# Fill products on TensorE and re-spaced side work in a tile-by-tile cross attention

## The reference

```python
q = (x @ Wq + bq).reshape(1, B * N, H, hd)          # 1024 queries, 16 heads of 16
kv = (cond @ Wkv + bkv).reshape(1, -1, 2, H, hd)    # 1024 keys, all batches together
q = _fq_sym(q * scale, axis=-1)     # scale 1/4; rounded to 255 steps per row and head
k = _fq_sym(k, axis=-1)
v = _fq_sym(v, axis=2)
attn = softmax(einsum('bhqd,bhkd->bhqk', q, k))
attn = _fq_unsigned(attn, axis=-1)  # rounded to 256 steps of the row's maximum
out = einsum('bhqk,bhkd->bhqd', attn, v)
return out.reshape(B, N, C) @ Wp + bp
```

## Time and profile before

| | |
|---|---|
| median of 3 executions | 662.7 us (661.12 to 663.51) |
| the profiled execution, its own time | 660.63 us |
| its span | 658.7 us |
| TensorE matmuls busy | 468.4 us (71%) |
| VectorE busy | 455.1 us (69%) |
| ScalarE busy | 299.2 us (45%) |
| GpSimd busy | 269.0 us (41%) |
| mean granted TensorE clock | 0.723 |

### The profile page before, as it was taken

One profiled execution on the slowest core, in us unless ns is written; L12 is line 12 of the kernel. 1 busy time (PEld: TensorE's weight loads), 2 busy tenths in 40 slices (PEclk: granted clock), 3 DMA queues, 4 the chain that ended last, 5 costly groups with the idle time before them and its releaser, 6 DMA issues.

```text
span 658.7 us, 9547 instructions
## 1 busy us (share of the span) xinstructions
PE 468.4 (71%) x3244; PEld 263.3 (40%) x3244; DVE 455.1 (69%) x930; ACT 299.2 (45%) x526; POOL 269.0 (41%) x335
## 2 busy tenths in 40 slices
PE   2966825648888785989989989999995147555640
PEld 1525612436455553334343434343333136444430
DVE  6797999878469769897878887878893842211003
ACT  1453113544400644876767676767772103323320
POOL 6441659884250553032221212121110047888870
PEclk9988876977789998555565755565555557999885
DMA  8640000007000001979877896979997198885556
GB/s 306 186 158 1 0 0 1 0 12 117 1 1 1 2 3 33 173 133 159 136 145 151 143 159 132 153 141 162 167 162 187 22 321 211 200 218 91 86 68 205
DMA packets 187247, 74.87 MB, mean 114 GB/s; under 512 B 159232, under 2 KB 184768, under 8 KB 187200
## 3 DMA queue, kind: packets, MB, share of 16 engines
q1 hardware_dynamic: 181056, 65.35, 46.3%
q0 software_dynamic: 6144, 8.92, 7.7%
HBM read 27.56 MB, written 8.93 MB: 55 GB/s over the span
## 4 chain that ended last, share of the span: by engine, by line
PE 37%; DVE 36%; issue 9%; DMA 8%; POOL 5%; ACT 3%; SPq 0%; POOLq 0%; DVEq 0%; ACTq 0%
PE ps L968 9%; DVE nm L1356 8%; PE ps L907 5%; DMA sums<-A,slot_token 4%; DVE AT L1274 4%; PE ps L897 4%; PE ps L747 3%; PE ps L978 3%; DMA A<-x_rows,slot_token 3%; POOL A L571 2%; POOL sums L585 2%; PE ps L902 2%; PE ps L846 1%; PE ps L766 1%; DVE AT L1146 1%
## 5 line engine op out<-in xcount | busy, mean ns | idle before, releaser
L700 ACT ACTIVATE A<-ps,b,sq 128x1024 int16<-128x1024 f32 x128 | 154.0, 1203 | 72.1 <-DVE b L1360 66.8
L1356 DVE TENSOR_REDUCE nm<-ps 128x1 f32<-128x1024 f32 x128 | 155.4, 1214 | 7.9 <-PE ps L968 7.2
L968 PE MATMUL ps<-big,ctx_sb 64*128 64x512 bf16 x256 | 124.0, 587 | 15.0 <-ACT A L700 12.5
L978 PEld LDWEIGHTS ps<-VI,A 128*128 128x128 f16 x1024 | 37.2, 105 | 99.9 <-issue 94.9
L1466 DVE TENSOR_TENSOR AT<-AT,ps 128x128 f32<-128x128 f32 x32 | 9.2, 287 | 84.1 <-ACT AT L717 70.2
L519 POOL TENSOR_SCALAR veps<-mv 128x1 f32<-128x1 f32 (+1 forms) x15 | 3.5, 233 | 149.2 <-DVE mv L1288 149.2
L585 POOL DMA_INDIRECT sums<-A,slot_token x32 | 51.5, 1608 | 15.4 <-issue 8.6
L978 PE MATMUL ps<-VI,A 128*128 128x16 f16 x1024 | 48.6, 176 | 3.8 <-DMA A<-A 3.8
L571 POOL DMA_INDIRECT A<-x_rows,slot_token x32 | 34.5, 1078 | 32.6 <-DVE slot_token L1456 23.1
L1047 PE MATMUL ps<-identf,A 128*128 128x128 f32 x64 | 15.3, 325 | 37.8 <-DMA A<-x_rows,slot_token 37.7
L711 ACT ACTIVATE A<-ps 128x256 f32<-128x256 f32 x32 | 12.2, 383 | 58.7 <-PE ps L1047 57.0
(11 more groups left out here) (271 smaller groups left out, 996.6 us busy)
## 6 DMA issues: line engine op xcount, KB each, us to landing
A<-in SPq DMA_DIRECT2D x32, 256.0 KB
A<-in SPq DMA_DIRECT2D x32, 128.0 KB
A<-in SPq DMA_DIRECT2D x2, 1024.0 KB, 14.8
sums<-zeros SPq DMA_DIRECT2D x4, 512.0 KB, 4.7
A<-A SPq DMA_TRANSPOSE x128, 3.3
A<-sums SPq DMA_DIRECT2D x8, 256.0 KB, 4.6
X<-in SPq DMA_DIRECT2D x1, 1024.0 KB, 5.8
big<-in SPq DMA_DIRECT2D x1, 1024.0 KB, 8.5
```

Source lines behind the costliest of these rows:

```text
L700: a.activation(Y5[:, n % YB, :], ps[:, 2 * (n % 3):2 * (n % 3) + 2, :], ACT.Exp, scale=sq5[:, q, h:h + 1], bias=b5[:, n % 4:n % 4 + 1], ac ...
L968: done = T.matmul(ps[:, 2 * (n % 3) + c, :], QT5[rows, q % 3, h // 2, :], KT5[rows, h // 2, c * 512:(c + 1) * 512], start=True, stop=True)
L978: done = T.matmul(ps[:, 6 + q % 2, h * HD:(h + 1) * HD], PT5h[:, m % YB, k, :], VI[:, k, h * HD:(h + 1) * HD], start=(k == 0), stop=(k == 7))
L1356: v.tensor_reduce(nm5[:, n % 4:n % 4 + 1], ps[:, 2 * (n % 3):2 * (n % 3) + 2, :].rearrange("p a c -> p (a c)"), AX.X, ALU.max, negate=True ...
```

## The change

- In each of the 128 units in which no side product is issued, TensorE makes two products of 256 columns of the identity with stored keys, into a part of a bank that nothing reads.
- The side products move. The order of a block was: transpose 1, wp 3, out_proj 5, transpose of tile q - 1 at 7, of tile q + 2 at 9, router 10, queries 12. It is now: transpose 2, out_proj 4, wp 6, transpose of tile q + 2 at 8, queries 10, transpose of tile q - 1 at 12, router 14. The order of the layer norms and of what GpSimd and SyncE do follows it.
- The bias of the queries is added by a product of one row on TensorE ahead of the query projection; ScalarE copies the queries and the logits out of PSUM, which VectorE did before.
- The factor 1/4 is left out of the reciprocal and multiplied into the scale, on GpSimd for tiles 2 to 7, and the first head of a tile waits for it on VectorE and ScalarE.

The diff (left out: the order of the layer norms, the declaration of LG5 in a free part of A, and its use by the router):

```diff
@@ -282,11 +283,12 @@
             q, rest = (n - LAG5) // H, (n - LAG5) % H
             return q if n >= LAG5 and rest == h else None
 
-        AT_H, WP_H, WO_H, X5_H, X4_H, LG_H, Q5_H = 1, 3, 5, 7, 9, 10, 12
+        AT_H, WO_H, WP_H, X4_H, Q5_H, X5_H, LG_H = 2, 4, 6, 8, 10, 12, 14
         SIDE5 = []
         for q in range(NT + 1):
-            SIDE5 += [("at", q - 1), ("wp", q - 1)] * (q >= 1) + [("wo", q + 2)] * (q + 2 < NT) + [("x5", q - 1)] * (q >= 1)
-            SIDE5 += [("x4", q + 2)] * (q + 2 < NT) + [("lg", q - 1)] * (q >= 1) + [("q5", q + 2)] * (q + 2 < NT)
+            done, ahead = q >= 1, q + 2 < NT
+            SIDE5 += [("at", q - 1)] * done + [("wo", q + 2)] * ahead + [("wp", q - 1)] * done + [("x4", q + 2)] * ahead
+            SIDE5 += [("q5", q + 2)] * ahead + [("x5", q - 1)] * done + [("lg", q - 1)] * done
         SIDE_READ = {"at": "at5T_ready", "wp": "xp_ready", "wo": "xo_ready", "x5": "x5T_ready", "x4": "x4T_ready", "lg": "lg_ready", "q5": "uq5_ready"}
 
         def wait_side_read(eng, i):
@@ -384,15 +386,16 @@
                 if n >= YB:
                     sp.wait_ge(S["p5V_done"], n - YB + 1)
                 sp.dma_start_transpose(PT5[:, n % YB, :, :], Y5[:, n % YB, :]).then_inc(p5T_loaded[n % YB], 16)
-                q = at_unit(n, X5_H + 1)
+                q = at_unit(n, 10)
                 if q is not None and q >= 1:
                     store_rows(q - 1)
-                q = at_unit(n, Q5_H + 3)
+                q = at_unit(n, 14)
                 if q is not None and q + 2 < NT:
                     query_T(q + 2)
             sp.wait_ge(S["p5V_done"], U5)
             for e in range(4):
                 load_weights(e)
+            store_rows(NT - 2)
             store_rows(NT - 1)
             sp.wait_ge(S["router_ready"], 2)
             sp.dma_start(x_rows[0:DUMP, D:ROW].rearrange("(t p) e -> p t e", p=P), L6[:, :, 0:NE]).then_inc(S["rows_ready"], 16)
@@ -540,28 +543,26 @@
                 if n in (21, 23):
                     add_bp((n - 21) // 2)
 
-            for n in range(U5 + LAG5 + H):
-                q = at_unit(n, WP_H + 1)
-                if q is not None and q >= 1:
+            for q in range(NT + 1):
+                if q + 2 < NT:
+                    ln_rstd("q", q + 2, q + 3)
+                    ln_apply("q", q + 2)
+                    add_bp(q + 2)
+                if q >= 1:
                     ln_rstd("r", q - 1, q)
                     if q < NT:
                         ln_apply("r", q - 1)
-                q = at_unit(n, WO_H + 1)
-                if q is not None and q + 2 < NT:
+                if q + 2 < NT:
                     t = q + 2
-                    ln_rstd("q", t, t + 1)
-                    ln_apply("q", t)
-                    add_bp(t)
-                q = at_unit(n, Q5_H + 2)
-                if q is not None and q + 2 < NT:
-                    t = q + 2
-                    pool.wait_ge(S["q5_step"], 5 + 4 * (t - 1))
+                    c = 8 * NT + 3 * q
+                    pool.wait_ge(S["q5_step"], 5 + 3 * (q + 1))
+                    g.tensor_scalar(sq5[:, t, :], sq5[:, t, :], 0.25, None, ALU.mult).then_inc(S["kq_step"], 1)
                     heads = AT[:, t, :].rearrange("p (h d) -> p h d", d=HD)
                     scaled = ktmp[:, 0, :].rearrange("p (h d) -> p h d", d=HD)
                     g.tensor_tensor(scaled, heads, rq5[:, t, :].unsqueeze(2).to_broadcast([P, H, HD]), ALU.mult).then_inc(S["kq_step"], 1)
-                    pool.wait_ge(S["kq_step"], 8 * NT + 2 * (t - 2) + 1)
+                    pool.wait_ge(S["kq_step"], c + 2)
                     g.tensor_scalar(kpart[:, t, :, 0, :], scaled, ROUND, -ROUND, ALU.add, ALU.add).then_inc(S["kq_step"], 1)
-                    pool.wait_ge(S["kq_step"], 8 * NT + 2 * (t - 2) + 2)
+                    pool.wait_ge(S["kq_step"], c + 3)
                     g.tensor_copy(kpart[:, t, :, 1:3, :], kpart[:, t, :, 0:1, :].to_broadcast([P, H, 2, HD])).then_inc(S["q5i_ready"], 1)
 
             def gather(e):
@@ -674,27 +675,34 @@
                         side_copy(t, bank4("xT", 1), t * D, "x4T_ready")
 
             for n in range(U5 + LAG5 + H):
-                q = at_unit(n, AT_H)
-                if q is not None and q >= 1:
+                q = (n - LAG5) // H
+                bank = 6 + (q + 1) % 2
+                if at_unit(n, AT_H) is not None and q >= 1:
                     act.wait_ge(S["at5T_psum"], q)
                     if q >= 2:
                         act.wait_ge(S["lg_psum"], q - 1)
                     else:
                         act.wait_ge(S["q5_psum"], 1)
-                    side_copy(0, 6 + (q + 1) % 2, 0, "at5T_ready")
-                q = at_unit(n, X5_H)
-                if q is not None and q >= 1:
+                    side_copy(0, bank, 0, "at5T_ready")
+                if at_unit(n, X4_H) is not None and q + 2 < NT:
+                    act.wait_ge(S["x4T_psum"], q + 3)
+                    act.wait_ge(S["q5_psum"], q + 2)
+                    side_copy(1, bank, 0, "x4T_ready")
+                if at_unit(n, Q5_H) is not None and q + 2 < NT:
+                    act.wait_ge(S["q5_psum"], q + 3)
+                    a.activation(AT[:, q + 2, :], ps[:, bank, 0:D], ACT.Copy).then_inc(S["uq5_ready"], 1)
+                if at_unit(n, X5_H) is not None and q >= 1:
                     act.wait_ge(S["x5T_psum"], q)
                     act.wait_ge(S["wp_psum"], q)
-                    side_copy(0, 6 + (q + 1) % 2, D, "x5T_ready")
-                q = at_unit(n, X4_H)
-                if q is not None and q + 2 < NT:
-                    act.wait_ge(S["x4T_psum"], q + 3)
-                    act.wait_ge(S["q5_psum"], q + 2)
-                    side_copy(1, 6 + (q + 1) % 2, 0, "x4T_ready")
+                    side_copy(0, bank, D, "x5T_ready")
+                if at_unit(n, LG_H) is not None and q >= 1:
+                    act.wait_ge(S["lg_psum"], q)
+                    a.activation(LG5[:, q - 1, :], ps[:, bank, D:D + NROUTE], ACT.Copy).then_inc(S["lg_ready"], 1)
                 if n < U5:
                     h, q = n % H, n // H
                     act.wait_ge(S["bias5_ready"], n + 1)
+                    if h == 0 and q >= 2:
+                        act.wait_ge(S["kq_step"], 8 * NT + 3 * (q - 2) + 1)
                     if n >= YB:
                         act.wait_ge(p5T_loaded[n % YB], 16 * (n // YB))
                     a.activation(Y5[:, n % YB, :], ps[:, 2 * (n % 3):2 * (n % 3) + 2, :], ACT.Exp, scale=sq5[:, q, h:h + 1],
@@ -902,9 +910,11 @@
                     last = T.transpose(ps[:, bank, lo + k * P:lo + (k + 1) * P], source[:, k * P:(k + 1) * P], identf[:, :])
                 last.then_inc(S[done], 1)
 
-            def side_project(slot, w, cols, bank, lo, done):
+            def side_project(slot, w, cols, bank, lo, done, bias=None):
+                if bias is not None:
+                    T.matmul(ps[:, bank, lo:lo + cols], onesf[0:1, :], bias[0:1, :], start=True, stop=False)
                 for k in range(KD):
-                    last = T.matmul(ps[:, bank, lo:lo + cols], XTs[:, slot, k, :], w[:, k, 0:cols], start=(k == 0), stop=(k == KD - 1))
+                    last = T.matmul(ps[:, bank, lo:lo + cols], XTs[:, slot, k, :], w[:, k, 0:cols], start=(k == 0 and bias is None), stop=(k == KD - 1))
                 last.then_inc(S[done], 1)
 
             pe.wait_ge(S["w_loaded"], 16 * 10)
@@ -957,6 +967,7 @@
             pe.wait_ge(S["vint_ready"], 2 * NT)
             side = 0
             for n in range(U5 + LAG5 + H):
+                before = side
                 if n < U5:
                     h, q = n % H, n // H
                     if h == 0:
@@ -984,36 +995,40 @@
                     pe.wait_ge(S["o5_ready"], q)
                     side_T(AT[:, q - 1, :], bank, 0, "at5T_psum")
                     side += 1
+                if at_unit(n, WO_H) is not None and q + 2 < NT:
+                    wait_side_read(pe, side - 1)
+                    wait_pos(pe, S["o5_ready"], q)
+                    pe.wait_ge(S["on4_ready"], 4 * ((q + 2) // 2 + 1))
+                    out_proj(q + 2, bank, 0)
+                    side += 1
                 if at_unit(n, WP_H) is not None and q >= 1:
                     wait_side_read(pe, side - 1)
                     pe.wait_ge(S["vscale_ready"], 6)
                     side_project(0, wp5, D, bank, D, "wp_psum")
                     side += 1
-                if at_unit(n, WO_H) is not None and q + 2 < NT:
+                if at_unit(n, X4_H) is not None and q + 2 < NT:
                     wait_side_read(pe, side - 1)
-                    pe.wait_ge(S["on4_ready"], 4 * ((q + 2) // 2 + 1))
-                    out_proj(q + 2, bank, 0)
+                    pe.wait_ge(S["xn_ready"], 4 * NT + ln("q", q + 2))
+                    side_T(XN[:, q + 2, :], bank, 0, "x4T_psum")
+                    side += 1
+                if at_unit(n, Q5_H) is not None and q + 2 < NT:
```

(39 more changed lines are left out.)

9 lines of the change are left out of this document (5 added, 4 removed).

## The result

The changed kernel takes 681.4 us (median of four, 674.95 to 681.52) against 663.1 for the kernel before: a ratio of 1.0255, 95% interval 1.019 to 1.032. It is slower by 18 us. The span of the profiled execution is 679.5 us, against 658.7.

A forecast was written before the change was run, and what follows sets the result against it. VectorE sets the pace only just, with 0.10 us spare on TensorE at half clock. Five full blocks +8.9, first +4.5, block without projection +3.7, last units +1.4: +18.5 us on 660.6, 679.1, by the median 681.2; range 657 to 693.

The forecast's parts named there:

- The 2.1 us that I added: Whole kernel: the median of the kernel before lay 2.1 us above its profiled execution, turning 679.1 into 681.2 us.
- the part behind the units: Drain after the last unit: no filler and the same order of the chain, so 0, within +-1 us.
- The filled unit: Units without a side product: 1.71 us on TensorE at half clock against VectorE's 1.38; at full clock 1.04, hidden.
- their 0.10 us spare: Clean units before the change, half clock: TensorE needs 1.28 us, VectorE 1.38, so only 0.10 us is free.
- Side products: TensorE start to start, half clock: transposes 1.78 us, router 2.30, output projection 3.19, out_proj 4.89, queries with bias 4.15.
- the upper bound that I gave it: One-row bias product in the query unit: between 0 and 0.96 us at half clock, taken as 0.96.
- time which TensorE pays anyway: Query unit: at half clock, ScalarE's wait for the projection falls within TensorE's 4.15 us and adds nothing.
- The clock: Units 5 to 8, after each out_proj: 6.8 us at full clock, gaining 1.84 us a full block.
- that case: Full block whose clock never rises: 35.26 us; as a rival for every block, 691 us in all, chance 0.10.
- the edge of what I had named: Sign against the forecast: the clock falling somewhere other than two to three units behind the output's projection.
- The blocks: Full block 33.4 us, first 32.3, without a projection ahead 29.6, last nine units 16.9; together +18.5 us.
- The reason for the clock: Cross-attention units: 64-row score products hold the clock weakly, and the filler is too small beside them to prolong it.

## Why the prediction was right

Forecast 681.2, measured 681.4. So close a hit is partly luck. The sum of the units was right, 18.5 us forecast and 18.9 measured. The 2.1 us that I added because the profiled execution of the kernel before lay under its median did not recur in the changed kernel, whose profiled execution is at its median; in their place the part behind the units grew by 2.1. By steps:

- **The filled unit.** 1.71 us at half clock forecast, 1.72 measured; at full clock 1.38 on VectorE, hidden, as said. But TensorE did not fall into VectorE's pace with 0.3 us idle in each unit: it ran ahead (from 310.43 to 311.51 a filled unit took 1.08 us) until the score buffers were full, and then idled 1.32 us at once, just ahead of the query unit. The sum of the fillers, by the run without them, is 23 us, and the earlier trace rows with their 0.10 us spare were the right place to look.
- **Side products,** TensorE start to start at half clock, forecast in brackets: transposes 1.80 us (1.78), out_proj 4.89 (4.89), router product 2.23 (2.30), output projection 3.19 (3.19). At full clock the unit with the output projection took 1.79 on TensorE and 2.38 on VectorE, whose 1.38 + 1.03 I had counted. The query unit took 4.41 against 4.15.

The query unit on the timeline of the changed kernel, all engines. The first two lines are the score pair of the unit with the output projection and the one behind it:

```profile
311.51 0.60 PE L979 MATMUL ps<-big,ctx_sb 64*128 64x512 bf16 x2
...
313.30 0.60 PE L979 MATMUL ps<-big,ctx_sb 64*128 64x512 bf16 x2
...
318.21 1.01 PE L979 MATMUL ps<-big,ctx_sb 64*128 64x512 bf16 x2 [1.32 <-ACT A L708]
...
319.46 1.22 PE L915 MATMUL ps<-bqr,onesf 1*128 1x256 f32 x2
...
320.61 2.08 PE L917 MATMUL ps<-wq,A 128*128 128x256 f32 x4
...
322.62 1.03 PE L979 MATMUL ps<-big,ctx_sb 64*128 64x512 bf16 x2
...
322.72 0.38 ACT L693 ACTIVATE AT<-ps 128x256 f32<-128x256 f32 x1 [1.90 <-PE ps L917]
...
323.69 1.22 DVE L1370 TENSOR_REDUCE nm<-ps 128x1 f32<-128x1024 f32 x1 [2.81 <-PE ps L979]
```

The two records of the bias product take 1.15 us to the next start, not 0.96: the product of which no row existed lies above the upper bound that I gave it. VectorE then waits 2.81 us for the next scores, and ScalarE 1.90 ahead of its copy. That this wait was on time which TensorE pays anyway was right.

- **The clock.** 6.8 us at full in five blocks, as taken. I let it rise in all six; in the block from 366.1 it did not, and this block took 35.6 us (35.3 forecast for that case). In the first block it was full for 6.8 us instead of 3.4, which gave back 1.1. The two errors cancel to about 1 us. The clock fell between units 9 and 10, three to four units behind the output projection, at the edge of what I had named, and in all five blocks before the one-row product started: with two fillers that product is not what ended the stretch.
- **The blocks.** Full 33.2 with the clock's stretch (33.4), first 31.1 (32.3), without a projection ahead 29.6 (29.6), last units 17.1 (16.9), 18.9 us more in all (18.5).
- **Not in the sum.** The part behind the units is 2.1 us longer, with no filler in it. I had it within 1 us; which of its parts moves it, no run here separates. Over all the kernels above it lies between 162.4 and 165.5 us, and the two ends have the same work in it.
- **The reason for the clock.** That the fillers were too small beside products of 64 rows was argued from stretches that lay far apart. The runs bear it out: with no filler or two the clock was full for 6.8 us at a time, with four for up to 34.1, and with the same four and a bias product of 128 instead of 1 row for up to 40.5. With enough in each unit it holds from 276 to 426 us. What I did not see is that the change itself brings in work that ends the full clock once the fillers are large enough to hold it until there, a product of one row.
- **What my sum hid.** I had no term for the gain of the re-spacing. It was there, 0.5% by the run without filler: the output projection now comes two units behind out_proj, at the clock that out_proj has raised, and the transposes of the next tile too. It is inside the 6.8 us that I took for the clock. Without any filler these 6.8 us are the same.

## What to carry to other kernels

Fill work on TensorE costs its full time where TensorE is the bound or near it at half clock, and it pays only if it holds the clock: here too little of it, spread over all units, cost 23 us, and more of it, placed only behind the product that had raised the clock, in the re-spaced kernel and with the bias product on 128 rows, took 32 us off the kernel before. Before adding such work, compare at half clock the start-to-start time of TensorE with that of the engine that sets the pace; the difference (0.10 us here) is all that is free. And look at the rows that a product contracts: a one-row product that saved another engine 0.4 us ended the full clock here, with four fillers, in five of six blocks, in three of them until the next out_proj or for good.

## What the runs showed of the hardware

- A float32 product of one row takes TensorE as long as one of 128 rows (0.69 and 0.68 us in two records at full clock), though the unit around it was 0.29 us longer. In the kernel with four fillers the clock fell in five of the six units with the one-row product and in none of the six with 128 rows: 683.7 against 658.0 us. With transposes as filler it went through five of six, and in four of these fell in the unit behind.
- Float32 transposes as filler held the clock about as products did (23.6 us at a time; mean clocks 0.746 to 0.829 against 0.745 to 0.786).
- Products from the lower and upper 64 rows, issued one behind the other and independent, overlap: units of 1.39 and 2.04 us in turn on VectorE, instead of the 2.14 of TensorE that four fillers on 128 rows took.
- An idle gap of 0.99 us did not end the full clock, in the kernel with four fillers and the bias product on 128 rows.
- The times of one and the same kernel can lie far apart (transposes as filler), and go with the mean granted clock: 648.7 us at 0.829, 664.7 at 0.799, 670.3 at 0.795, 690.7 at 0.746. Where in the kernel the clock fell differently is not shown, since only one of them has a profile.
